# Padding the low product of f2 to 36 rows, with new instruction orders on all five engines

## The reference

```python
# layer 0, per batch: self attention (sa), cross attention (ca), MLP; 16 heads of 16
h = x + attention(rms(x), rms(x), wq, wk, wv, wo)
h = h + attention(rms(h), ctx, ca_wq, ca_wk, ca_wv, ca_wo)
h = h + (silu(rms(h) @ w_gate) * (rms(h) @ w_up)) @ w_down      # inner 1024
# layer 1, query h, features ctx
norm_F = layernorm(h); norm_X = layernorm(ctx)
attended = softmax(norm_F @ norm_X.T / 16) @ norm_X
g = gelu(attended @ fc1_w.T + fc1_b)                            # 4 values a row
cross = g @ fc2_w.T + fc2_b                                     # 4 -> 256: "f2"
nc = layernorm(cross); self_att = softmax(nc @ nc.T / 16) @ nc
out = norm_F + gamma2 * (cross + gamma1 * self_att)
```

## Time and profile before

| | |
|---|---|
| median of three runs | 1123.17 us (1122.73 to 1124.32) |
| the profiled execution | 1123.86 us |
| its span, first to last instruction | 1122.1 us |
| PE busy | 999.5 us (89%), 8556 matmuls |
| weight loads (PEld) busy | 820.9 us (73%) |
| DVE, ACT, POOL busy | 672.6 (60%), 623.4 (56%), 249.0 (22%) us |
| mean granted TensorE clock | 0.945 of full speed |

### The profile page before, as it was taken

The page is one execution under the profiler, slowest core; times in us unless marked ns, Lnnn a source line. Parts: engine busy times, 40 slices in busy tenths (PEclk is TensorE's granted clock), DMA queues, the critical chain, the costliest instruction groups (busy, mean ns, idle before and its releaser), DMA issues.

```text
span 1122.1 us, 22714 instructions
## 1 busy us (share of the span) xinstructions
PE 999.5 (89%) x8556; PEld 820.9 (73%) x8556; DVE 672.6 (60%) x1509; ACT 623.4 (56%) x1318; POOL 249.0 (22%) x306
## 2 busy tenths in 40 slices
PE   2576889899999999999999999999999999989764
PEld 1455677778788787878787787878887878777652
DVE  3624364758576675758485856667575848565542
ACT  4243446474756665665647465756567574845332
POOL 4000011112213131413132221213141312231332
...
DMA packets 68868, 63.65 MB, mean 57 GB/s; under 512 B 17156, under 2 KB 64173, under 8 KB 68784
## 3 DMA queue, kind: packets, MB, share of 16 engines
...
...
## 4 chain that ended last, share of the span: by engine, by line
PE 71%; DVE 13%; ACT 6%; issue 6%; DMA 2%; POOL 1%; SPq 1%; ACTq 0%; DVEq 0%; POOLq 0%
PE mring L928 16%; PE ring L928 15%; PE down_ps L1071 7%; PE od L1021 7%; DVE mx_sa L773 6%; PE ring L1007 5%; PE ring L987 4%; PE mring L1135 3%; PE ring L1033 2%; ACT probs L631 2%; PE ring L936 2%; PE mring L1081 2%; PE ring L1041 1%; PE mring L1098 1%; DVE xn_a L746 1%
## 5 line engine op out<-in xcount | busy, mean ns | idle before, releaser
L631 ACT ACTIVATE probs<-ring 128x1024 f32<-128x1024 f32 (+1 forms) x192 | 190.6, 1023 | 24.0 <-PE ring L1007 22.3
L502 POOL TENSOR_TENSOR hidT_lo<-hid,hidT_hi 128x256 fp32r<-128x256 f32 x128 | 93.9, 739 | 457.4 <-ACT hidT_hi L660 457.4
L773 DVE TENSOR_REDUCE mx_sa<-ring 128x4 f32<-128x1024 f32 x128 | 152.8, 1219 | 14.8 <-PE ring L987 14.8
L815 DVE SCALAR_TENSOR_TENSOR hid<-hid,mring 128x256 f32<-128x256 f32 x128 | 53.1, 415 | 84.9 <-ACT hid L652 84.8
L778 DVE TENSOR_REDUCE mx_ca<-ring 128x4 f32<-128x308 f32 x128 | 55.4, 475 | 78.2 <-PE ring L987 77.4
L652 ACT ACTIVATE hid<-mring 128x256 f32<-128x256 f32 x128 | 48.7, 380 | 83.2 <-PE mring L928 83.2
L987 PE MATMUL ring<-pk_sa 63*128 63x256 f32 x512 | 67.9, 347 | 27.7 <-DVE mx_sa L773 15.7
L987 PEld LDWEIGHTS ring<-pk_sa 63*128 63x128 f32 x512 | 41.3, 199 | 51.2 <-DVE mx_sa L773 16.0
L1071 PE MATMUL down_ps<-down_hi,hidT_hi 128*128 128x256 f32 x256 | 77.2, 302 | 0.0
L1021 PE MATMUL od<-probs,vz_sa 128*32 128x256 f32 x1024 | 76.8, 400 | 0.1
L1071 PE MATMUL down_ps<-down_lo,hidT_hi 128*128 128x256 f32 x256 | 72.5, 283 | 0.0
...
## 6 DMA issues: line engine op xcount, KB each, us to landing
...
```

Source lines behind the costliest of these rows:

```text
L502: nc.gpsimd.tensor_tensor(hidT[1][:, m % HID, :], hid[:, m % 2, :], hidT[0][:, m % HID, :].bitcast(F32), ALU.subtract).then_inc(S["hidlo"] ...
L631: nc.scalar.activation(granule(g, tag)[0:rows_, i0:i0 + 2, :, :].rearrange("p i h t -> p h i t"), ring_tile(("E", tag, k))[0:rows_].rearra ...
L773: nc.vector.tensor_reduce(mx[tag][:, :, :, k].rearrange("p q h -> p h q"), ps[:].rearrange("p h (q t) -> p h q t", t=T), AX_X, ALU.max).th ...
L815: nc.vector.scalar_tensor_tensor(out=hid[:, m % 2, :], in0=hid[:, m % 2, :], scalar=1.0, in1=ps[:, 0:T], op0=ALU.add, op1=ALU.mult).then_i ...
```

## The change

The tensor of low weights gets 36 rows like the one of high weights; DVE sets it to zero first, and the low matmul of f2 reads all 36 rows of g_r. Row for row the added products are with zero. The lists of ORDER are laid out afresh on all five engines; no step is added or removed.

```diff
--- before.py
+++ after.py
@@ -47,30 +47,30 @@
 
 ORDER = {
     "sp": """
-        wl.10@1 ldr@0 wl.2@5 ldcl@-1 wl.4@4 pqk.sa.1@1 mr.sa@1 pq.ca@0 wl.9@2 pk.ca@0 wl.0@6 st@-3 wl.5@3 wl.1@6 mr.ca@0 ldx@3 pqk.sa.0@2 ldc@1 wl.6@3 wl.7@3
-        wl.8@3 wl.3@5
+        ldr@1 wl.10@1 wl.0@6 ldcl@-1 ldc@1 mr.sa@1 wl.9@2 wl.7@3 pk.ca@0 wl.1@6 pq.ca@0 mr.ca@0 wl.8@3 wl.5@4 wl.2@5 ldx@3 wl.3@5 wl.6@4 pqk.sa.0@2 wl.4@5
+        st@-3 pqk.sa.1@2
     """,
     "pool": """
-        lnstat.nc@-2 hi.5@-1 hi.6@-1 hi.7@-1 ms.mlp@0 ms.ca@1 bF@-2 hi.0@0 lnstat.nf@-1 hi.1@0 bC@-2 hi.2@0 ms.sa@3 hi.3@0 lnstat.nx@0 hi.4@0
+        lnstat.nc@-2 hi.5@-1 hi.6@-1 bF@-2 hi.7@-1 ms.mlp@0 ms.ca@1 hi.0@0 lnstat.nf@-1 hi.1@0 lnstat.nx@0 bC@-2 ms.sa@3 hi.2@0 hi.3@0 hi.4@0
     """,
     "act": """
-        hi.5@-2 E.ca.0@-1 o.sa.1@0 E.ca.1@-1 E.ca.2@-1 gu.7@-2 ws.6@3 nCT@-3 E.ca.3@-1 o.ca.0@-1 cT.ca@0 aT.sa@0 o.ca.1@-1 hi.6@-2 v.ca@0 ws.9@1 ws.3@4 ws.0@5
-        hi.7@-2 ws.1@5 s2e@-3 aT.ca@-1 nXT@-2 p2T@-3 norm.mlp@-1 h1@0 norm.ca@0 T.mlp@-1 v.sa@1 gu.0@-1 ws.7@2 T.ca@0 ws.10@1 ws.4@4 maxT.sa@1 ws.5@4 ws.2@5
-        hi.0@-1 gu.1@-1 norm.sa@2 qk.ca@0 gu.2@-1 hi.1@-1 E.sa.0@1 E.sa.1@1 gu.3@-1 nFT@-2 hi.2@-1 E.sa.2@1 E.sa.3@1 E.sa.4@1 hi.3@-1 sce@-2 E.sa.5@1 gu.4@-1
-        gu.5@-1 o.sa.0@1 E.sa.6@1 pT@-2 E.sa.7@1 hi.4@-1 ws.8@2 h4@-2 T.sa@2 maxT.ca@0 f2@-2 gu.6@-1 qk.sa@2
+        nCT@-3 E.ca.2@-1 E.ca.3@-1 o.ca.0@-1 cT.ca@0 ws.9@1 ws.10@1 ws.7@2 aT.sa@0 o.ca.1@-1 v.ca@0 hi.7@-2 aT.ca@-1 s2e@-3 p2T@-3 norm.mlp@-1 h1@0 norm.ca@0
+        T.mlp@-1 v.sa@1 nXT@-2 T.ca@0 gu.0@-1 norm.sa@2 ws.0@6 maxT.sa@1 hi.0@-1 gu.1@-1 ws.2@5 qk.ca@0 hi.1@-1 ws.3@5 gu.2@-1 E.sa.0@1 ws.4@4 gu.3@-1
+        E.sa.1@1 E.sa.2@1 ws.6@3 nFT@-2 E.sa.3@1 hi.2@-1 E.sa.4@1 sce@-2 gu.4@-1 ws.8@2 E.sa.5@1 ws.5@4 hi.3@-1 E.sa.6@1 gu.5@-1 pT@-2 E.sa.7@1 ws.1@6
+        o.sa.0@1 h4@-2 T.sa@2 hi.4@-1 maxT.ca@0 f2@-2 gu.6@-1 hi.5@-1 o.sa.1@1 qk.sa@2 E.ca.0@0 hi.6@-1 gu.7@-1 E.ca.1@0
     """,
     "dve": """
-        maxsplit.ca@-1 glo@-3 ws.6@2 T.sa@1 ws.2@4 lnstat.nc@-3 gu.6@-2 qk.sa@1 lncen.nc@-3 lncen.nx@-2 ws.3@4 gu.7@-2 oT.sa@0 cT.ca@0 aT.sa@0 ws.4@4 s2@-3
-        ws.8@1 oT.ca@-1 ws.9@1 wo.sa@0 p2T@-3 ws.0@5 S.sa.0@1 aT.ca@-1 dn@-2 S.sa.1@1 wo.ca@-1 S.sa.2@1 S.sa.3@1 ms.mlp@-1 S.sa.4@1 xn.mlp@-1 ms.ca@0 pv2@-3
-        S.sa.5@1 ws.5@4 T.mlp@-1 xn.ca@0 S.sa.6@1 S.sa.7@1 maxsplit.sa@1 T.ca@0 gu.0@-1 lnstat.nf@-2 gu.1@-1 qk.ca@0 lncen.nf@-2 ws.10@1 gu.2@-1 gu.3@-1
-        lnstat.nx@-1 out@-3 ms.sa@2 sc@-2 S.ca.0@0 scn@-2 ws.7@2 gu.4@-1 S.ca.1@0 gu.5@-1 ws.1@5 xn.sa@2 S.ca.2@0 S.ca.3@0
+        S.ca.3@-1 maxsplit.ca@-1 glo@-3 T.sa@1 lnstat.nc@-3 lncen.nx@-2 gu.6@-2 qk.sa@1 lncen.nc@-3 gu.7@-2 ws.4@4 oT.sa@0 cT.ca@0 aT.sa@0 s2@-3 oT.ca@-1
+        ws.8@1 ws.0@6 wo.sa@0 aT.ca@-1 S.sa.0@1 dn@-2 S.sa.1@1 ws.1@6 p2T@-3 ws.3@5 wo.ca@-1 S.sa.2@1 S.sa.3@1 ms.mlp@-1 S.sa.4@1 xn.mlp@-1 ws.9@1 ms.ca@0
+        pv2@-3 S.sa.5@1 T.mlp@-1 xn.ca@0 ws.10@1 S.sa.6@1 S.sa.7@1 maxsplit.sa@1 ws.5@4 T.ca@0 gu.0@-1 ws.2@6 lnstat.nf@-2 ms.sa@2 gu.1@-1 ws.7@2 lncen.nf@-2
+        qk.ca@0 ws.6@4 gu.2@-1 lnstat.nx@-1 gu.3@-1 sc@-2 out@-3 scn@-2 gu.4@-1 xn.sa@2 S.ca.0@0 gu.5@-1 S.ca.1@0 S.ca.2@0
     """,
     "pe": """
-        dnp.2@-2 qk.sa@1 dnp.3@-2 dnp.4@-2 E.ca.0@-1 pv.sa.3@0 E.ca.1@-1 E.ca.2@-1 gu.7@-2 nCT@-3 oT.sa@0 E.ca.3@-1 pv.ca.0@-1 s2@-3 cT.ca@0 aT.sa@0
-        pv.ca.1@-1 v.ca@0 nXT@-2 oT.ca@-1 wo.sa@0 dnp.5@-2 S.sa.0@1 aT.ca@-1 dnp.6@-2 dnp.7@-2 S.sa.1@1 wo.ca@-1 S.sa.2@1 p2T@-3 S.sa.3@1 S.sa.4@1 pv2@-3
-        S.sa.5@1 T.mlp@-1 v.sa@1 S.sa.6@1 S.sa.7@1 gu.0@-1 T.ca@0 gu.1@-1 maxT.sa@1 qk.ca@0 gu.2@-1 dnp.0@-1 E.sa.0@1 E.sa.1@1 gu.3@-1 nFT@-2 E.sa.2@1
-        E.sa.3@1 pv.sa.0@1 sc@-2 E.sa.4@1 gu.4@-1 E.sa.5@1 S.ca.0@0 pv.sa.1@1 gu.5@-1 S.ca.1@0 E.sa.6@1 dnp.1@-1 pT@-2 E.sa.7@1 S.ca.2@0 h4@-2 pv.sa.2@1
-        S.ca.3@0 T.sa@2 gu.6@-1 maxT.ca@0 f2@-2
+        qk.sa@1 dnp.3@-2 E.ca.0@-1 gu.7@-2 E.ca.1@-1 oT.sa@0 nCT@-3 dnp.4@-2 E.ca.2@-1 pv.ca.0@-1 E.ca.3@-1 s2@-3 cT.ca@0 aT.sa@0 pv.ca.1@-1 v.ca@0 oT.ca@-1
+        wo.sa@0 aT.ca@-1 dnp.5@-2 S.sa.0@1 dnp.6@-2 dnp.7@-2 S.sa.1@1 wo.ca@-1 S.sa.2@1 p2T@-3 S.sa.3@1 S.sa.4@1 pv2@-3 S.sa.5@1 T.mlp@-1 v.sa@1 nXT@-2
+        S.sa.6@1 S.sa.7@1 gu.0@-1 T.ca@0 gu.1@-1 maxT.sa@1 qk.ca@0 gu.2@-1 E.sa.0@1 gu.3@-1 E.sa.1@1 E.sa.2@1 nFT@-2 dnp.0@-1 E.sa.3@1 dnp.1@-1 pv.sa.0@1
+        E.sa.4@1 sc@-2 gu.4@-1 E.sa.5@1 E.sa.6@1 pv.sa.1@1 gu.5@-1 S.ca.0@0 dnp.2@-1 pT@-2 E.sa.7@1 S.ca.1@0 h4@-2 S.ca.2@0 S.ca.3@0 gu.6@-1 T.sa@2 pv.sa.2@1
+        maxT.ca@0 f2@-2 pv.sa.3@1
     """,
 }
 
@@ -159,7 +159,7 @@
         fc1b_sb = sb("fc1b_sb", [FC, 1])
         LO_AT = 32
         fc2_hi = sb("fc2_hi", [LO_AT + FC, D], F32R)
-        fc2_lo = sb("fc2_lo", [FC + 1, D], F32R)
+        fc2_lo = sb("fc2_lo", [LO_AT + FC, D], F32R)
 
         ident = sb("ident", [P, P])
         half_neg = sb("half_neg", [P, QT])
@@ -717,9 +717,11 @@
             nc.vector.memset(half_neg[:], -0.5).then_inc(s_vset, 1)
             nc.vector.memset(g_r[:].bitcast(F32), 1.0).then_inc(s_vset, 1)
             nc.vector.memset(fc2_hi[:].bitcast(F32), 0.0).then_inc(s_vset, 1)
+            nc.vector.memset(fc2_lo[:].bitcast(F32), 0.0).then_inc(s_vset, 1)
+            dve.wait_ge(s_vset, 4)
             dve.wait_ge(s_small, 16 * N_SMALL)
             dve.wait_ge(s_fc2, 2)
-            nc.vector.tensor_tensor(fc2_lo[:], fc2_staged[0:FC + 1], fc2_hi[0:FC + 1].bitcast(F32), ALU.subtract).then_inc(s_fc2, 1)
+            nc.vector.tensor_tensor(fc2_lo[0:FC + 1], fc2_staged[0:FC + 1], fc2_hi[0:FC + 1].bitcast(F32), ALU.subtract).then_inc(s_fc2, 1)
 
             def split_w(n, k):
 
@@ -899,7 +901,7 @@
         def _(pe):
             mm = nc.tensor.matmul
             pe.wait_ge(s_small, 16 * N_SMALL)
-            pe.wait_ge(s_vset, 3)
+            pe.wait_ge(s_vset, 4)
             for k in range(len(ROWS)):
                 last = mm(ring[k // 4][:, (k // 2) % 2, (k % 2) * D:(k % 2 + 1) * D], ones_row, row_of(k), start=True, stop=True)
             last.then_inc(s_bcmm, 1)
@@ -1120,7 +1122,7 @@
                 ps = mfill(n, "f2")
                 for q in range(QT):
                     mm(ps[:, q * D:(q + 1) * D], g_r[:, q * P:(q + 1) * P], fc2_hi[:], start=True, stop=False)
-                    last = mm(ps[:, q * D:(q + 1) * D], g_r[0:FC + 1, q * P:(q + 1) * P], fc2_lo[:], start=False, stop=True)
+                    last = mm(ps[:, q * D:(q + 1) * D], g_r[:, q * P:(q + 1) * P], fc2_lo[:], start=False, stop=True)
                 last.then_inc(S["f2"].sem, 1)
 
             def t_nC(n):
```

## The result

| | before | after |
|---|---|---|
| time, median of 7 runs each | 1123.47 us | 1130.40 us |
| lowest to highest | 1122.73 to 1124.48 | 1127.29 to 1132.58 |
| ratio, 95% interval | | 1.0053 [1.0038, 1.0069] |
| profiled execution (span) | 1123.86 (1122.1) | 1130.47 (1128.7) |

The change makes the kernel slower by 0.5%; forecast was 0.4% faster. From here "before" and "after" are the two kernels, and lines of after are two higher than those of before (L1124 and L1125 are f2, L1009 the E fills).

What follows compares the result with a forecast made beforehand. PE was taken as the bound, 97% busy at 61 us a batch. Steady part -0.5, start +0.5 and end -4.0 sum to -4.0 us from the profiled 1123.86, so 1119.2 us by the median, range 1110 to 1127.

Steps and rivals of the forecast that it cites:

- f2: Four f2 matmuls on PE: equal height brings their starts closer and shortens the exit, gaining 0.58 us a batch.
- Rival D: Slower, 1126.3 us, chance 0.18: weight loads into rows still in use, not height changes, keep f2's starts 0.31 apart.
- Extra boundaries: PE's new order: six more changes of matmul height between neighbouring steps, costing 0.95 us a batch.
- (a): PE at the E.ca fills: the third fill's wait for the first one's exponential goes, -0.9 us a batch.
- (e): PE at oT.ca: nXT no longer covers the copy of o.ca.1, +0.05 us a batch.
- (c): PE at oT.sa, second ring fill after E.ca.0: new wait for that fill's exponential, +0.6 us a batch.
- (d): PE at S.ca.2, second fill after E.sa.7: new wait for that fill's exponential, +0.3 us a batch.
- (b): PE's small waits between S.sa.2 and T.ca: nXT fills one, bF's move shortens xn.ca, -0.48 us a batch.
- bF: POOL base product moved earlier, off the DVE normalizations: 0.30 us a batch for PE and 2.07 at the end.
- End: Last batches: shorter xn.mlp, two cheaper f2 fills and no E.ca wait, -4.0 us, bounds -1 and -6.
- Start: First batches: moved splits delay maxT by 2 us, mostly regained through pv.sa.3's place, +0.5 us, bounds -3 and +3.
- splits of up and down: DVE in batch 0, moved behind S.sa.4 and S.sa.5: first hidden by v.sa, second delays maxT by 2 us.

Runs made afterwards that it cites:

- pad_only: The kernel before with only the 36-row padded low product, all orders as before: 1114.01 us, ratio 0.9911 to before.
- order_only: The changed kernel's new orders with the old 5-row low product: 1138.42 us, ratio 1.0118 to before.
- pad_bF: pad_only with one POOL step, bF, moved ahead of hi.7, ms.mlp and ms.ca: 1107.15 us, ratio 0.9851 to before.
- pad_bF_ca: pad_bF with E.ca.0 and E.ca.1 together on PE, then pv.sa.3, gu.7, E.ca.2: 1107.20 us, ratio 0.9850 to before.
- splits_back: The changed kernel with the two splits of up and down on DVE back in their old places: 1128.77 us, ratio 1.0035 to before.
- e6_only: The changed kernel with pv.sa.1 ahead of the E.sa.6 fill on PE, in the first passes only: 1125.29 us, ratio 1.0008 to before.
- ca_start: pad_bF_ca with pv.sa.3 put back between E.ca.0 and E.ca.1 in the first passes only: 1101.77 us, ratio 0.9821 to before.
- new_start: splits_e6 with pv.sa.3 of batch 1 moved to between E.ca.0 and E.ca.1 of batch 0: 1122.99 us, ratio 1.0000 to before.
- splits_e6: The changed kernel with the repairs of both splits_back and e6_only: 1122.23 us, ratio 0.9987 to before.

## Why the prediction was wrong

It gave 1119.2 us, 1110 to 1127, faster at 0.56; measured are 1130.4 us. Point by point:

- **f2** (-0.58 a batch): 0.55 by pad_only. Rival D is out, since the second start came down to 0.22. The rule of the Trainium skill that the prediction cited (TensorEngine Tiling (Array Packing), Tiling Modes, Key Properties), a drain at each change of tiling mode, agrees with this part: starts 0.31 us apart came to 0.22 and 0.12 when the changes of height went. The orders, which have six such changes more, lost 0.49 a batch net of all waits; what the changes alone cost there no run shows.
- **Extra boundaries and the waits (a) to (e)** (+0.52 a batch in sum): 0.49 by order_only. Two terms were also measured by themselves: (c) 0.51 for 0.6, (d) 0.22 for 0.3. For (b), the part from bF is 0.39 by pad_bF, where I took 0.30. Wait (a), 0.9, is gone in after; removed in another way, by pad_bF_ca, it gave 0.34 net of a new wait of 0.3. That the terms are right singly and not only in sum is thus shown for f2, (c), (d) and bF, and not for the boundaries.
- **End** (-4.0, bounds -1 and -6): -5.5. Inside the bounds, but not by its terms, so this is in part luck. The padding was priced at 1.2 there and measures 3.8 (152.0 to 148.2, pad_only). One piece of that is seen: the last f2 runs at the low clock, where its starts were 0.51, 0.50 and 0.51 us apart and are now 0.38, 0.21 and 0.22, a gain of 0.7 for the three distances alone. The bF term was priced at 2.1 and leaves 1.2 (pad_bF). With the low product of 5 rows the new orders alone take 4.4 off the end (order_only), so the parts sum to more than the whole.
- **Start** (+0.5, bounds -3 and +3): +12.9. This is the step that failed. It counted the splits of up and down, rightly (it said 2 us of maxT, splits_back shows 1.6), and took pv.sa.3 ahead of the next qk.sa as a gain. In the first pass that order is no gain: the chain above shows pv.sa.3 as half of the 2.82 us directly ahead of the qk.sa of batch 1, though no run prices it by itself. And it left out three things.

First, the order was read as a cycle, and the first pass is not the cycle: with the cross-attention of batch -1 absent, E.sa.7 takes the tile of E.sa.6, and pv.sa.1 stands behind that fill. This costs 2.6 us at the next qk.sa (e6_only). Second, the term had no price for the clock. Before and after differ by 17.1 us of low clock up to 300 us; at half rate this is at most 8.5 of the 12.9 us, less where PE waits anyway. Third, E.ca.0 and E.ca.1 are neighbours in batch 0, since the gu.7 between them has no batch to belong to; E.ca.1 then waits 1.7 us where before waited 0.7. In pad_bF_ca and ca_start that one place is worth 5.4 us of the end time, nearly all through the clock. In after the same stretch is 4.6 us longer than in before; that it is the same cause there is likely from the same wait, the same fall and the fourteen profiles above, and new_start, where the fall is gone from this place, shows that it is not free to undo.

Together the chain, the splits and the clock behind them account for 9.4 of the 12.9 us by the profile of splits_e6, one of its shortest runs, and for 8.2 by its median. Its f2 of batch 0 is then 3.5 us behind that of before, still just outside the bound of 3 that I had given; the rest is open. The last sentence of the prediction named this place as the weak one, and the range did not act on it: bounds of 3 us either way, for a stretch in which PE's granted clock is 0.6 to 0.7 and every wait shows, came from the size of the moved instructions alone.

Three slips in the working changed nothing: twelve periods of -0.06 are -0.7 and not -0.5; 0.17 and 0.08 give a lower price of 0.25 for a parting and not 0.28; and E.sa.1 and E.sa.2 are still a pair in the new order.
